# Gated attention and expert FFN on one core: the long convolution's outer products move to VectorE, its low parts to GpSimd

## The reference, cut to what matters

```python
# v = layernorm(x); x1 = x2 = ctx; rows of 256 are 32 heads H of 8 (num_heads)
kv  = vr[:, :, :, None, :] * x2r[:, :, None, :, :]      # 8 x 8 outer product per head and position
y   = irfft(rfft(kv, 1024) * rfft(k, 1024))[..., :512]  # causal convolution along the sequence
y   = y + kv * skip                                     # skip[h, i]
out = einsum('bhijl,bhil->bhjl', y, x1r)                # sum over i of y[i, j] * x1[i]
x   = x + tanh(g_xattn) * out
```

## Time and profile before

| | |
|---|---|
| median of 3 runs | 799.68 us (796.83 to 801.11) |
| the profiled execution | 799.75 us, its span 797.5 us |
| stages 0 to 2 of the convolution | 36.6 to 106 us of the span |
| stages 3 to 15 | 106 to 376 us |
| routing and FFN | 381 us to the end |
| TensorE busy | 84% of the span |
| GpSimd busy | 77%, in 140 to 340 us nearly all of the time |

### The profile page before, as it was taken

How to read it: one execution, slowest core, us unless ns; L and a number is a source line. 1 busy time by engine, 2 the same in 40 slices (tenths; PEclk the granted TensorE clock), 3 DMA queues, 4 the chain that set the end, 5 groups by cost and what they waited for, 6 DMA issues and landing times.

```text
span 797.5 us, 11004 instructions
## 1 busy us (share of the span) xinstructions
PE 670.8 (84%) x3136; PEld 540.1 (68%) x3137; DVE 527.9 (66%) x661; ACT 241.9 (30%) x348; POOL 617.8 (77%) x373
## 2 busy tenths in 40 slices
PE   1387779888888989986781989999999999999974
PEld 0366668666666767765671767888788888888863
DVE  4259768777777777775742999559897983650400
ACT  4123313333333333322321222333233233223320
POOL 3399979999999999991273669779888886875862
PEclk9998889999999999998696899999999999999996
DMA  4999375555554544410496676446666664541110
GB/s 136 353 347 312 133 213 145 145 145 145 145 145 145 145 145 132 118 55 26 157 223 171 231 246 222 172 143 201 208 231 201 198 223 128 188 132 41 50 51 6
DMA packets 58462, 130.63 MB, mean 164 GB/s; under 512 B 5932, under 2 KB 6124, under 8 KB 58448
## 3 DMA queue, kind: packets, MB, share of 16 engines
q1 hardware_dynamic: 43108, 96.87, 38.8%
q10 hardware_dynamic: 11020, 20.99, 8.1%
q0 software_dynamic: 4320, 12.60, 6.0%
HBM read 111.11 MB, written 37.67 MB: 187 GB/s over the span
## 4 chain that ended last, share of the span: by engine, by line
PE 36%; DVE 7%; POOL 3%; issue 3%; DMA 2%; ACT 0%; DVEq 0%; POOLq 0%; ACTq 0%
PE pair L1197 21%; PE bank L1210 12%; POOL sorted_x L937 2%; PE bank L1230 2%; DMA sorted_x<-xn_all,pos 1%; DVE up L1023 1%; DVE down_hi L1023 1%; DVE down_lo L1026 1%; DVE gate L1023 1%; DVE up L1026 1%; PE bank L1186 1%; DVE gate L1026 1%; DMA raw<-down_w 1%; DVE select L876 0%; POOL ys L1131 0%
## 5 line engine op out<-in xcount | busy, mean ns | idle before, releaser
L742 PE MATMUL bank<-kv_hi,strip 128*128 128x512 f32 x640 | 222.4, 415 | 24.2 <-DMA strip<-strips 22.3
L742 PEld LDWEIGHTS bank<-kv_hi,strip 128*128 128x128 f32 x640 | 125.4, 196 | 55.1 <-issue 26.2
L325 POOL TENSOR_TENSOR kv<-vT,cK 128x2048 f32<-128x2048 f32 x31 | 156.1, 5036 | 0.0
L742 PE MATMUL bank<-kv_lo,strip 128*128 128x512 f32 x320 | 131.0, 409 | 0.0
L621 DVE TENSOR_TENSOR kv_lo<-kv,kv_hi 128x2048 fp32r<-128x2048 f32 x32 | 81.5, 2548 | 51.6 <-ACT kv_hi L519 51.5
L462 POOL TENSOR_TENSOR prod<-prod 128x1024 f32<-128x1024 f32 x31 | 107.5, 3487 | 4.7 <-DVE prod L634 4.7
L1197 PE MATMUL pair<-gate,xT_hi 128*128 x304 | 98.9, 407 | 5.0 <-DVE xT_lo L1032 2.8
L1197 PE MATMUL pair<-up,xT_hi 128*128 x304 | 96.7, 399 | 2.8 <-DVE up L1026 2.8
L634 DVE TENSOR_TENSOR prod<-bank,cT 128x512 f32<-128x512 f32 x128 | 82.1, 681 | 25.4 <-DMA cT<-ctx_cols 20.7
L1023 DVE CAST down_hi<-raw 128x1024 fp32r<-128x1024 f32 x32 | 34.2, 1068 | 73.7 <-PE bank L1210 50.5
L519 ACT ACTIVATE kv_hi<-kv 128x2048 fp32r<-128x2048 f32 x32 | 61.3, 1916 | 65.8 <-POOL kv L325 54.8
(11 more groups left out here) (149 smaller groups left out, 1131.1 us busy)
## 6 DMA issues: line engine op xcount, KB each, us to landing
strip<-strips SPq DMA_DIRECT2D x16, 1024.0 KB, 5.7
raw<-gate_w SPq DMA_DIRECT2D x32, 512.0 KB, 4.1
raw<-up_w SPq DMA_DIRECT2D x32, 512.0 KB, 4.4
raw<-down_w SPq DMA_DIRECT2D x32, 512.0 KB, 4.3
strips<-kparts ACTq DMA_DIRECT2D x1, 12288.0 KB, 74.7
sorted_x<-fill SPq DMA_DIRECT2D x14, 513.0 KB, 6.0
xs<-sorted_x ACTq DMA_DIRECT2D x20, 256.5 KB
x_in<-x_rows SPq DMA_DIRECT2D x16, 256.0 KB, 5.5
```

Of the source, the lines that this page charges most:

```text
L325: engine.tensor_tensor(kv[:, hh, :].rearrange("p (a i j) -> p a i j", i=J, j=J), v.unsqueeze(3).broadcast_to([P, LB * NB, J, J]), c.unsque ...
L742: last = nc.tensor.matmul(y_bank[lb][:, :], strip[:, u, 2 * hh + t, d * P:(d + 1) * P], v[:, u, hh, mb * COL:(mb + 1) * COL], start=(mb == ...
```

## The change

It reassigns the steps around kv and the skip term, and reorders the queues to match.

- `vT` and ScalarE's copy into it are gone. `outer` runs on VectorE and reads v from `v_bank` in PSUM; both heads of stage g + 1 are formed in stage g, the first behind `skip_sum(g)`, the second behind `add_fours(g - 1)`. `outer` waits for `s_vtr`, the context, and for `s_khi`, `s_klo` and `s_skip` of two heads before.
- `kv_low` runs on GpSimd.
- `skip_first` multiplies the diagonal of `kv` (32 x 8 numbers, each 9 from the next) by skip, once per head, in place of two products of 512.
- `add_pairs` adds both heads in one contiguous instruction of 2048, so it waits for the last product of its stage. `skip_last(g)` moves from GpSimd's stage g to its stage g + 1, behind `add_pairs(g)`. For the last stage, `add_first_pairs` (GpSimd) and `add_last_pairs` (VectorE) do a head each.
- `skip_sum` moves from the second head's products of the stage before to a place behind the first two products of its own stage; `ln1` behind the first product of the second head.
- GpSimd's `before_conv` now is, for each head, `skip_first` and `kv_low`.
- `xn2` has two buffers, and ScalarE's copies of it move (`xn2T_out` a stage later, `xn2_out` of the last stage ahead of the last copy of logits). `v_in` moves behind the last block of the second head.

The core of the diff: first `outer` on VectorE, then GpSimd's functions and its `stage`, last VectorE's `stage`.

```diff
+                def outer(g, u, n, hh):
                     h = 2 * g + hh
+                    if hh == 0:
+                        dve.wait_ge(s_vtr, g + 1)
+                        dve.wait_ge(s_cK[u], 16 * (n + 1))
+                    wait(dve, s_khi, h - 1)
+                    wait(dve, s_klo, h - 1)
+                    wait(dve, s_skip, h - 1)
+                    v = v_bank.rearrange("p (a r) -> p a r", r=2 * J)[:, :, hh * J:(hh + 1) * J]
+                    c = cK[:, u, :].rearrange("p (a r) -> p a r", r=2 * J)[:, :, hh * J:(hh + 1) * J]
+                    nc.vector.tensor_tensor(
+                        kv[:, hh, :].rearrange("p (a i j) -> p a i j", i=J, j=J),
+                        v.unsqueeze(3).broadcast_to([P, LB * NB, J, J]),
+                        c.unsqueeze(2).broadcast_to([P, LB * NB, J, J]), ALU.mult).then_inc(s_kv, 1)
...
+                def skip_first(g, u, hh):
+                    eng.wait_ge(s_kv, h + 1)
                     wait(eng, s_skw, g)
+                    same = kv[:, hh, :].rearrange("p (a d) -> p a d", d=J * J)[:, :, ::J + 1]
+                    nc.gpsimd.tensor_tensor(v, same, s_g.unsqueeze(1).broadcast_to([P, LB * NB, J]), ALU.mult)\
+                        .then_inc(s_skip, 1)
+                def kv_low(g, u, hh):
+                    eng.wait_ge(s_khi, h + 1)
+                    nc.gpsimd.tensor_tensor(kv_lo[:, u, hh, :], kv[:, hh, :], kv_hi[:, u, hh, :].bitcast(f32),
+                                            ALU.subtract).then_inc(s_klo, 1)
+                def add_pairs(g, u):
+                    eng.wait_ge(s_p, (g + 1) * 2 * LB)
+                    nc.gpsimd.tensor_tensor(prod[:, u, 0:J // 2, :], prod[:, u, 0:J // 2, :],
+                                            prod[:, u, J // 2:J, :], ALU.add).then_inc(s_add, 1)
...
                 def stage(g, u, n):
                     if known(g, lambda g: g >= 1):
-                        add_pairs(g - 1, 1 - u, 1)
-                    skip_last(g, u, n)
+                        add_pairs(g - 1, 1 - u)
+                        skip_last(g - 1, 1 - u, n - 1 + u)
                     if known(g, lambda g: g < G - 1):
-                        before_conv(g + 1, 1 - u, n + u)
-                    add_pairs(g, u, 0)
+                        before_conv(g + 1, 1 - u)
...
                     product(g, u, n, 0, 0)
                     product(g, u, n, 0, 1)
+                    skip_sum(g)
+                    if more:
+                        outer(g + 1, 1 - u, n + u, 0)
+                    product(g, u, n, 0, 2)
                     if before:
                         add_fours(g - 1, 1 - u)
-                    if known(g, lambda g: g < G - 2):
-                        ln1(g + 2, u, n + 1)
-                    product(g, u, n, 0, 2)
+                    if more:
+                        outer(g + 1, 1 - u, n + u, 1)
                     product(g, u, n, 0, 3)
                     if before:
                         residual(g - 1, 1 - u, n - 1 + u)
                         ln2_first(g - 1, 1 - u)
-                    if more:
-                        kv_low(g + 1, 1 - u, 0)
-                    if before:
                         ln2_last(g - 1)
                     product(g, u, n, 1, 0)
+                    if known(g, lambda g: g < G - 2):
+                        ln1(g + 2, u, n + 1)
                     product(g, u, n, 1, 1)
-                    if more:
-                        skip_sum(g + 1)
                     product(g, u, n, 1, 2)
                     product(g, u, n, 1, 3)
-                    if more:
-                        kv_low(g + 1, 1 - u, 1)
```

More of the change, by code:

```diff
@@ L151, in flamingo_layer_kernel @@
     xn = put("xn", [P, L], f32, att)
-    xn2 = put("xn2", [P, L], f32, att)
+    xn2 = put("xn2", [P, 2, L], f32, att)
     xn2T = put("xn2T", [P, LB, P], f32, att)
-    vT = put("vT", [P, 2, LB * P], f32, att)
     cT = put("cT", [P, 2, LB * P], f32, att)
@@ L342, in load_cK @@
                     wait(eng, s_kv, 2 * (g - 1))
-                    wait(eng, s_skip, g - 1)
                     eng.dma_start(cK[:, u, :], rows(ctx_cols, g)).then_inc(s_cK[u], 16)
@@ L456, in skip_last, with add_first_pairs, before_conv @@
                         .then_inc(s_skp, 1)
-                def add_pairs(g, u, hh):
-                    eng.wait_ge(s_p, (2 * g + hh + 1) * LB)
-                    terms = prod[:, u, 0:J, :].rearrange("p i (a r) -> p i a r", r=2 * J)[:, :, :, hh * J:(hh + 1) * J]
+                def add_pairs(g, u):
+                    eng.wait_ge(s_p, (g + 1) * 2 * LB)
+                    nc.gpsimd.tensor_tensor(prod[:, u, 0:J // 2, :], prod[:, u, 0:J // 2, :],
+                                            prod[:, u, J // 2:J, :], ALU.add).then_inc(s_add, 1)
+                def add_first_pairs(g, u):
+                    eng.wait_ge(s_p, g * 2 * LB + LB)
+                    terms = prod[:, u, 0:J, :].rearrange("p i (a r) -> p i a r", r=2 * J)[:, :, :, 0:J]
                     nc.gpsimd.tensor_tensor(terms[:, 0:J // 2], terms[:, 0:J // 2], terms[:, J // 2:J], ALU.add)\
                         .then_inc(s_add, 1)
-                def before_conv(g, u, n):
-                    if isinstance(g, int) and g == 0:
-                        eng.wait_ge(s_small, 32)
-                        eng.wait_ge(s_kv, 1)
-                    else:
-                        outer(g, u, n, 0)
-                    skip_first(g, u)
-                    outer(g, u, n, 1)
+                def before_conv(g, u):
+                    for hh in range(2):
+                        if isinstance(g, int) and g == 0 and hh == 0:
+                            eng.wait_ge(s_small, 32)
+                        skip_first(g, u, hh)
+                        kv_low(g, u, hh)
                 def stage(g, u, n):
                     if known(g, lambda g: g >= 1):
-                        add_pairs(g - 1, 1 - u, 1)
-                    skip_last(g, u, n)
+                        add_pairs(g - 1, 1 - u)
+                        skip_last(g - 1, 1 - u, n - 1 + u)
                     if known(g, lambda g: g < G - 1):
-                        before_conv(g + 1, 1 - u, n + u)
-                    add_pairs(g, u, 0)
-                before_conv(0, 0, 0)
+                        before_conv(g + 1, 1 - u)
+                before_conv(0, 0)
                 stages(eng, stage)
+                skip_last(G - 1, 1, G // 2 - 1)
+                add_first_pairs(G - 1, 1)
             @block.scalar
@@ L500, in norm2, with xn2_out @@
                     act.wait_ge(s_nb2, g + 1)
-                    wait(act, s_x2tr, g)
-                    wait(act, s_xnc, g)
-                    norm(xn2[:, :], x_res[:, u, :], rs2, nb2, s_xn2)
+                    wait(act, s_x2tr, g - 1)
+                    wait(act, s_xnc, g - 1)
+                    norm(xn2[:, u, :], x_res[:, u, :], rs2, nb2, s_xn2)
+                def xn2_out(g, u):
+                    act.wait_ge(s_xn2, g + 1)
+                    nc.scalar.activation(xn_all[:, blk(g), 0:L].rearrange("p o n -> p (o n)"), xn2[:, u, :],
+                                         ACT.Copy).then_inc(s_xnc, 1)
                 def k_high():
@@ L661, in add_fours @@
                 def add_fours(g, u):
-                    dve.wait_ge(s_add, 2 * (g + 1))
+                    dve.wait_ge(s_add, G + 1 if isinstance(g, int) and g == G - 1 else g + 1)
                     nc.vector.tensor_tensor(prod[:, u, 0:2, :], prod[:, u, 0:2, :], prod[:, u, 2:4, :], ALU.add)\
@@ L727, in v_in @@
                     pe.wait_ge(s_xn, g + 1)
-                    wait(pe, s_vT, g)
-                    transposes(v_bank, xn, s_vtr)
+                    wait(pe, s_kv, 2 * g)
+                    transposes(v_bank, lambda cols: xn[:, cols], s_vtr)
                 def conv(g, u, n, hh, blocks):
@@ L767, in sum_heads, with x2_in @@
                     last.then_inc(s_att, 1)
-                def x2_in(g):
+                def x2_in(g, u):
                     pe.wait_ge(s_xn2, g + 1)
                     wait(pe, s_xn2T, g)
-                    transposes(x2T_bank, xn2, s_x2tr)
+                    transposes(x2T_bank, lambda cols: xn2[:, u, cols], s_x2tr)
                 def stage(g, u, n):
```

88 lines of the change are left out of this document (23 added, 65 removed).

## The result

The changed kernel is slower: 815.27 us, median of 4 runs (813.58 to 816.78), against 800.39 us for the kernel before on the same chip. The ratio is 1.0202, interval 1.0169 to 1.0234. The forecast was 800.2 with a range to 810; the time lies above the range. The profiled execution took 814.24 us, its span is 812.5.

What follows compares the result with a forecast made beforehand. GpSimd was taken to set the stage period of 20.77 us. Counted from stage 3, five stages of 20.17 and six of 21.23 gave +0.9, the tail -0.5, together +0.4 on 799.75: 800.2 us, range 792 to 810.

Steps and rivals of the forecast that it cites:

- that load: Load of cT, awaited 7.66 us by stage 3's first product at 106.28; claimed that earlier gains are lost there.
- Other edits, at nothing: Earlier ln1, xn2's second buffer and v_in's place: claimed to lie under VectorE's and TensorE's waits, costing nothing.
- the ring: Each stage: skip_sum awaits the previous skip plane, behind add_pairs, which awaits the previous last product; 20.17 us against 20.77.
- The walk: One stage timed on each engine from skip_sum to the next: GpSimd's path last, 20.17 us without a low clock.
- Rival D: A higher price in the stages: dearer GpSimd instructions, about 812 us, or outer taking turns with GpSimd, 816; chance 0.15.
- The clock: TensorE at half pace behind one wait of 2.2 to 2.8 us before sum_heads: 6 low stages of 11, 21.23 us each.
- all 11 would be low: TensorE falling to the low clock behind the wait of every stage, by the skill's rule; 805.5 us, chance 0.25.
- Rival C: TensorE's clock low in every stage, or its path always binding: 11 x 21.23, 805.5 us; chance 0.25.
- The outer product from PSUM: VectorE's outer, reading v from PSUM, expected at 2.28 us without taking turns with GpSimd.
- The second half of rival D: VectorE's outer takes turns with GpSimd's subtraction: +2.0 us a stage, 816 us; called small, within a chance of 0.15.
- The tail: Behind the last stage's sum_heads: the same until ScalarE's last copy, now ahead of the last logits; about -0.5 us.

Runs made afterwards that it cites:

- the added matmuls: Ten matmuls of 512 columns, result unread, ahead of each sum_heads, against the changed kernel with k_lo made first again: 802.87 us, ratio 1.0010.
- the first experiment: The changed kernel with k_lo made ahead of the first two layernorms again, as in the kernel before: 807.79 us, ratio 1.0091.

## Why the prediction was wrong

**The step that failed** is "Nothing in the change moves that load earlier: what stages 0 to 2 gain is lost in this wait. I count from there." It asked only whether stages 0 to 2 could gain. They lost 15.2 us at the first matmul, more than that wait holds, and skip_sum of stage 3 came at 118.5 for 107.5. The main cause, the call of `k_low()` behind two layernorms, is an edit that the prediction does not name; under "Other edits, at nothing" it lists an earlier ln1, which fits only these two calls (inside a stage ln1 moves to a later place), without asking what they now stand ahead of. Alone in the kernel before it costs 11.0 us by the medians (811.57 less 800.54), 8.2 of it in the trace up to sum_heads of stage 14, and undoing it in the changed kernel gives 7.5 back. Both runs show it.

**The second term that was mis-sized is the ring's period.** The ring was seen ("The new thing is a ring of waits") and walked in the right order: GpSimd's path last, TensorE's single wait, skip_sum waiting for the plane. The walk gave 20.17 us, the trace 20.86. The difference of 0.69 by its terms, each from the rows of the stage shown: kv and ScalarE's rounding 0.11 later than walked (5.09 from skip_sum to the subtraction, for 4.98); three instructions of 2048 at 4.57 from start to start, for 4.47: 0.3; skip_first at 0.88, for 0.67: 0.2; the plane to skip_sum 1.16, for 1.11. No wrong mechanism, but small terms that all lie on the same side; by twelve stages they are worth 8.3 us. Rival D had asked for a higher price, of skip_first at 1.25; it measured 0.82 to 0.93, and 4.49 to 4.66 for the 2048 lies inside the bounds of 3.7 and 4.68. Its 812 and 816 us stand next to the measured 815.3 by luck: neither of its costs came.

**The clock** came out near the forecast. Five of the twelve stages had a low stretch, for 7 (stage 3 and 6 of the other 11); such a stage takes 0.9 us more, for 1.06; the added matmuls took that away (4.9 us by the medians). The mechanism is the one of the walk: in the low stages the path through TensorE ends last. What does not hold is the ground that I gave for the count, that the length of the wait decides between full and half pace; the wait itself was 2.8 to 3.3 us, for 2.2 to 2.8. That the count came near is luck. The sums of 12 matmuls behind waits that are nearly equal, in the timeline of TensorE of the changed kernel:

```profile
123.57 2.77 PE L748 MATMUL pair<-ident,prod 128*128 128x128 f32 x12 [2.83 <-DVE prod L654]
145.34 1.53 PE L748 MATMUL pair<-ident,prod 128*128 128x128 f32 x12 [2.82 <-DVE prod L654]
...
187.02 1.53 PE L748 MATMUL pair<-ident,prod 128*128 128x128 f32 x12 [3.25 <-DVE prod L654]
207.83 1.74 PE L748 MATMUL pair<-ident,prod 128*128 128x128 f32 x12 [3.13 <-DVE prod L654]
229.54 2.82 PE L748 MATMUL pair<-ident,prod 128*128 128x128 f32 x12 [2.82 <-DVE prod L654]
```

Half and full pace behind 2.83 and 2.82, full pace behind 3.25. The Trainium skill (TensorE: Matmul & The Clock Gate, section on HAM oscillation) tells of a loop whose wait is longer than the work between two waits, and which falls back behind each. Here TensorE waits 3 us and works 17.5, so that it was the prediction that carried this over to "all 11 would be low", not the page; of the twelve stages seven stayed at full clock. Rival C, low in every stage, has the right side of the sign for another reason.

**The outer product from PSUM** does not take turns with GpSimd: 2.28 us at 166.02 while GpSimd's subtraction runs from 166.19. The second half of rival D is out. add_fours, with two operands in SBUF, starts at 164.50, inside skip_first, and takes 1.60 for its least of 1.22; it ends at 166.10, 1.08 after skip_first has ended (165.02), as in the earlier trace rows. The Trainium skill (GPSIMD Engine Reference, Specifications) has GpSimd's SBUF interfaces collide with VectorE instructions that read SBUF twice, and both durations agree.

**The tail** gave 2.0 us where 0.5 was forecast. 1.6 of it lie between the last sum and the first matmul of the routing, 12.19 us before and 10.60 now. In that stretch the kernel before runs partly at half pace, the changed one less so. The last sum before, in the changed kernel, and in the version with the added matmuls:

```profile
370.88 2.26 PE L764 MATMUL pair<-ident,prod 128*128 128x128 f32 x12 [1.19 <-DVE prod L664]
...
387.81 1.53 PE L748 MATMUL pair<-ident,prod 128*128 128x128 f32 x12 [1.19 <-DVE prod L654]
...
370.15 2.74 PE L748 MATMUL pair<-ident,prod 128*128 128x128 f32 x12 [1.19 <-DVE prod L654]
```

With the changed kernel's code behind the sum, but the sum at half pace, the version with the added matmuls takes 12.14 us for the same stretch. So about 1.1 us of the tail's 2.0 are the clock in these two executions; TensorE's last wait there is 0.5 shorter (2.16 us for 2.69), which is the forecast's 0.5.

**The sum again, with what was measured:** the forecast's +0.4; 11.0 at stage 3 (8.4 of it undone by the first experiment, 2.6 within the scatter of the load of cT); 5.0 in the stages (0.69 by 12 is 8.3, less 2.9, since seven low stretches at 1.06 were counted and five at 0.9 came: 5.4, of which 0.4 is not accounted for); -1.5 in the tail; -0.5 around the span (1.74 us, not 2.25). That is +14.4, and 814.24 less 799.75 is 14.5.

What the prediction did not ask is the more costly question: need the ring be there? It found a ring that leaves GpSimd idle for 4.3 us a stage, priced it, and took it as given. The ring's 3.2 us ahead of skip_first, with TensorE's low clock that comes of it, were worth 42 us, six times the late strips. With the ring open and `k_lo` early the change's steps make the kernel 4 to 5% faster than before (ratios 0.9526 and 0.9566); with it closed they make it 0.9% slower.

## What to carry to other kernels

Read every moved call of the prologue, however small: a subtraction of 0.67 us that comes 7.4 us late had a 1 MB transfer start beside one of 15 MB, and the first matmul came 17.4 us later in the kernel before (9.8 in the changed one). When a sum is counted from a point that waits for a load, ask both ways how far that point can move: here there were 7.7 us of slack, and of the 9.7 us beyond it 7.1 came through at stage 3.

Where several engines wait a like time in turn in each stage and none is full (three waits of 3.2 us, GpSimd busy 16.5 of 20.9), look for the ring and for the one link that needn't be there. A second buffer of 256 bytes, or an exchange of two neighbours in one queue, took the period from 20.8 to 17.6 us, without any instruction becoming faster.

## What the runs showed of the hardware

- TensorE's clock behind equal waits of 2.8 us is sometimes at full and sometimes at half pace (rows above), and it can fall within a stage whose sum began at full pace (207.83: 1.74 us for 1.53, with the granted clock of that stage at 0.92).
- GpSimd takes 0.82 to 0.93 us for 256 numbers per partition with a stride of nine, against 1.07 to 1.11 for 512 with another access pattern: half the size saves a fifth.
- The store of 256 KB that frees `x_res` took up to 14.7 us to land beside the 12 MB of strips (74.77 to 89.49), against 5.9 at the median of the three stores of the kernel before up to 125 us, all issued when the 12 MB had landed.
